# Attention maxima placed in two runs of 512 queries a unit, with earlier loads, column groups in the router and head copies in halves

## What is computed

```python
x = x + attention0(layernorm(x))     # 16 heads of 16, softmax over 1024 keys, k mixed from its two halves
x = x + ffn0(layernorm(x))           # 256 -> 1024 -> 256, ternary weights, a low-rank part, squared relu
x = x + statespace1(layernorm(x))    # a linear recurrence a feature, layernorm, gelu, projection
x = x + experts1(layernorm(x))       # 16 experts, the 2 best of each token, 256 -> 512 -> 256
```

```python
attn = jnp.einsum('bhqc,bhkc->bhqk', q, k_eff) * scale
attn = softmax(attn, axis=-1)
out  = jnp.einsum('bhqk,bhkd->bhqd', attn, v)
...
logits = jnp.einsum('sbd,de->sbe', x, Wg) + bg + bias
vals, idx = top_k(logits, 2)
```

## Time and profile before

| what | before |
|---|---|
| median of 3 runs | 1851.45 us (1850.39 to 1857.02) |
| the profiled execution | 1850.05 us, span in the profile 1848.3 us |
| projection, to the first matmul of attention | 0 to 122.2 us |
| attention | 122.2 to about 856 us |
| PE, DVE, ACT, POOL busy | 85%, 66%, 54%, 23% of the span |
| mean granted PE clock | 0.916 of full speed |

### The profile page before, as it was taken

How to read it: one execution, slowest core, us unless ns; L and a number is a source line. 1 busy time by engine, 2 the same in 40 slices (tenths; PEclk the granted TensorE clock), 3 DMA queues, 4 the chain that set the end, 5 groups by cost and what they waited for, 6 DMA issues and landing times. The chain is left out here.

```text
span 1848.3 us, 39878 instructions
## 1 busy us (share of the span) xinstructions
PE 1569.6 (85%) x13929; PEld 1028.1 (56%) x13930; DVE 1215.2 (66%) x2121; ACT 991.2 (54%) x2005; POOL 432.0 (23%) x569
## 2 busy tenths in 40 slices
PE   5949999999999999998789976889787299999990
PEld 4824333333333333334678865878674189888880
DVE  6639999999999999911478867666656822222225
ACT  2410888888888888883154422333223145554442
POOL 2119000000000000000112126222212355555550
PEclk9965999999999999997899986999897599999995
DMA  5682133333333443000100001332209432222118
GB/s 180 221 193 36 27 55 57 42 54 42 55 51 53 67 58 58 9 20 16 15 1 1 1 13 48 94 93 77 65 2 310 145 105 66 67 65 65 62 63 275
DMA packets 117613, 135.14 MB, mean 73 GB/s; under 512 B 27028, under 2 KB 91560, under 8 KB 117352
## 3 DMA queue, kind: packets, MB, share of 16 engines
q1 hardware_dynamic: 104712, 107.60, 25.1%
q0 software_dynamic: 7584, 20.72, 3.5%
q10 hardware_dynamic: 5184, 4.98, 0.8%
HBM read 92.23 MB, written 36.04 MB: 69 GB/s over the span
## 5 line engine op out<-in xcount | busy, mean ns | idle before, releaser
L1862 DVE TENSOR_REDUCE mx<-ps 128x1 f32<-128x1024 f32 x512 | 616.7, 1220 | 39.6 <-PE ps L1984 37.8
L1901 ACT ACTIVATE PR<-ps 128x512 f32<-128x512 f32 x1024 | 559.9, 595 | 140.3 <-PE ps L2026 74.3
L1984 PE MATMUL ps<-KQ 48*128 48x512 f32 x1024 | 393.3, 468 | 30.6 <-PEq L238 24.2
L2026 PE MATMUL ps<-KQ 50*128 50x512 f32 x1024 | 374.6, 445 | 0.0
L2010 PE MATMUL ps<-PR,VO 128*32 128x256 f32 x4096 | 328.2, 392 | 31.9 <-ACT OT L1891 31.5
L2026 PEld LDWEIGHTS ps<-KQ 50*128 50x128 f32 x1024 | 153.1, 186 | 211.0 <-ACT PR L1901 204.5
L2010 PEld LDWEIGHTS ps<-PR,VO 128*32 128x32 f32 x4096 | 81.7, 108 | 219.9 <-ACT PR L1901 121.1
L1984 PEld LDWEIGHTS ps<-KQ 48*128 48x128 f32 x1024 | 160.2, 196 | 60.8 <-DVE mx L1862 35.0
L1742 PE MATMUL ps<-eW,e_hiddenT 128*128 x632 | 155.4, 389 | 5.1 <-DVE e_hiddenT L1719 2.6
L1752 PEld LDWEIGHTS ps<-e_xinT,e_w 128*128 128x128 f32 x1264 | 154.9, 193 | 5.7 <-issue 1.7
L1752 PE MATMUL ps<-e_xinT,e_w 128*128 128x128 f32 x1264 | 155.5, 277 | 1.1 <-ACT e_xinT L1684 1.1
(11 more groups left out here) (276 smaller groups left out, 2160.0 us busy)
## 6 DMA issues: line engine op xcount, KB each, us to landing
KQ<-qk_parts SPq DMA_DIRECT2D x192, 128.0 KB, 6.0
qk_parts<-parts SPq DMA_DIRECT2D x8, 2048.0 KB, 6.9
TB<-toeplitz_lines SPq DMA_DIRECT2D x32, 512.0 KB, 5.5
eW<-in_L_ffn_W SPq DMA_DIRECT2D x16, 512.0 KB, 7.1
eW<-in_L_ffn_W SPq DMA_DIRECT2D x8, 1024.0 KB, 12.2
e_got<-expert_outputs SPq DMA_DIRECT2D x16, 512.0 KB, 10.2
X<-in_L_attn_x SPq DMA_DIRECT2D x8, 512.0 KB, 4.4
V<-OT SPq DMA_DIRECT2D x64, 64.0 KB, 6.5
```

What stands on the lines that cost most here:

```text
L1862: nc.vector.tensor_reduce(mx[:, u % RING, h * QT + q:h * QT + q + 1], ps[:, b:b + 2].rearrange("p a n -> p (a n)"), AX, ALU.max, negate=Tr ...
L1901: nc.scalar.activation(PR[:, kt % 2, h], ps[:, st_bank(u, s)], ACT.Exp).then_inc(exp_done, 1)
L1984: made = nc.tensor.matmul(ps[:, max_bank(u, t) + k], kq[half(h, KROWS), 1, h % HR, q * P:(q + 1) * P], kq[half(h, KROWS), 0, h % HR, k * B ...
L2026: nc.tensor.matmul(ps[:, st_bank(u, s)], kq[half(h, AROWS), 0, h % HR, kt * P:(kt + 1) * P], kq[half(h, AROWS), 1, h % HR, qc * BANK:(qc + ...
```

## The change

- **Early loads.** SP stores all chunks in one loop, and issues half of `load_qk` of unit 0 after the store of chunk 2 and the other half after chunk 3, and unit 1's after chunks 4 and 5. Nothing is left ahead of the stores of chunks 6 and 7.
- **Queries in two runs.** The query side of `KQ` is laid out by run of 512 queries, then head. `load_qk` has 6 transfers of 128 KB for the keys and 12 of 64 KB for the queries (pieces of 2 KB in place of 4 KB).
- **Maxima in two runs.** `negated_rows` comes after every 16th tile (`AHEAD`), for one run, on half as many columns. `rows(u, qc)` has 8 transfers of half the size for each run. PE waits for the rows of a run ahead of that run's first block. 16 + 12 tiles stand ahead of the first block of all. SP's order in a unit: `load_qk(u + 2)`, `heads(u - 1)`, `rows(u, 1)`, `rows(u + 1, 0)`, `spread_inverses`.
- **Heads in two copies.** `keep_heads` copies 256 queries at a time, after the first and the third exponential of the next step. PE waits for the first copy ahead of part 1 of the last step's `weigh`, and for both ahead of the next step's part 0.
- **Router in column groups.** `wg` is widened to 32 columns with zeros, which POOL writes ahead of its load. Each of a chunk's four token tiles has its own 32 partitions of the result (8 matmuls of 128 tokens in place of 2 of 512), ACT copies 128 x 128, and one matmul with 64 columns turns it back in place of four.

```diff
+                            FIRST_STORED = SEQ // CW
+                            for c in range(NC):
+                                h = c % 2
                                 sp.wait_ge(lo_ready, 2 * DK * (c + 2))
                                 sp.dma_start(pqk[...], parts[...]).then_inc(stored[h], 16)
-                            chunks(sp, body)
+                                u, second = divmod(c - FIRST_STORED, 2)
+                                if 0 <= u < 2:
+                                    for h2 in range(2):
+                                        sp.wait_ge(stored[h2], 16 * 2)
+                                    load_qk(sp, u, u, range(second * QK_LOADS // 2, (second + 1) * QK_LOADS // 2))
...
             for u in range(UNITS):
                 for t in range(MAXES):
                     reduce(u, t)
-                negated_rows(u)
+                    if (t + 1) % AHEAD == 0:
+                        negated_rows(u, t // AHEAD)
...
-                    if kt == 1 and h == 0:
-                        if step > KT:
-                            keep_heads(u, 0)
+                    if kt == 0 and h % 2 == 0:
+                        if step > 0:
+                            keep_heads(u, 0, h // 2)
                         elif u > 0:
-                            keep_heads(u - 1, 1)
+                            keep_heads(u - 1, 1, h // 2)
...
                 if u > 0:
                     heads(u - 1)
+                rows(u, 1)
                 if u + 1 < UNITS:
-                    rows(u + 1)
+                    rows(u + 1, 0)
...
+                kept_before = WPARTS * (QC * u + step // KT)
+                if kt == 0 and part == 0 and kept_before > 0:
+                    pe.wait_ge(ot_kept, kept_before)
+                if kt == KT - 1 and part > 0:
+                    pe.wait_ge(ot_kept, kept_before + part)
...
-            for t in range(MAXES + LEAD):
+            for t in range(AHEAD + LEAD):
...
-                    ahead = MAXES * (u + 1) + t + LEAD
+                    ahead = MAXES * u + AHEAD + t + LEAD
...
                         for dk in range(DK):
-                            last = nc.tensor.matmul(ps[0:E, 5 + h, 0:CW], wg[:, dk], xT[:, h, dk], ...)
+                            for k in range(CT):
+                                last = nc.tensor.matmul(ps[LANES * k:LANES * (k + 1), 5 + h, 0:P], wg[:, dk], xT[:, h, dk, k * P:(k + 1) * P], ...)
...
-                        for k in range(CT):
-                            last = nc.tensor.matmul(ps[:, 4, ds(E * (CT * c + k), E)], lT[h][:, k * P:(k + 1) * P], ident[0:E, 0:E], ...)
+                        nc.tensor.matmul(ps[:, 4, ds(CT * E * c, CT * E)], lT[h], lanes_of, ...)
```

More of the change, by code:

```diff
@@ L201, in transformer_kernel, with load_qk @@
                 KQ = [sbuf(st, f"KQ{r}", [P, 2, HR, SEQ], F32R) for r in range(2)]
+                queries = lambda r: KQ[r][:, 1].rearrange("p h n -> p (h n)").rearrange("p (b h n) -> p b h n", b=QC, n=BANK)
                 kq_loaded = [sem(f"kq_loaded{r}") for r in range(RING)]
-                def load_qk(sp, u, r):
+                K_LOADS = 2 * len(PAIR_K)
+                QK_LOADS = K_LOADS + QC * 2 * len(PAIR_Q)
+                def load_qk(sp, u, r, some=range(QK_LOADS)):
                     b, g = u // UPB, u % UPB
                     src = pqk.rearrange("s a k p t -> s a (k p) t").rearrange("s a (g h c) t -> s a g c h t", h=HG, c=HD)
[L208 to L213, removed]
+                    for n in some:
+                        j, y = n // 2 % len(PAIR_Q), n % 2
+                        row = HALF * y + HD * j
+                        if n < K_LOADS:
+                            to, side, part, start, width = KQ[r][row:row + HD, 0], 1, PAIR_K[j], 0, SEQ
+                        else:
+                            qc = n // K_LOADS - 1
+                            to, side, part, start, width = queries(r)[row:row + HD, qc], 0, PAIR_Q[j], BANK * qc, BANK
+                        sp.dma_start(to.bitcast(F32),
+                                     src[side, part, ds(g, 1), :, HR * y:HR * (y + 1), ds(SEQ * b + start, width)].rearrange("g c h t -> (g c) h t")).then_inc(kq_loaded[r], 16)
                 with ExitStack() as s1:
@@ L1578, in body @@
                         for dk in range(DK):
-                            last = nc.tensor.matmul(ps[0:E, 5 + h, 0:CW], wg[:, dk], xT[:, h, dk], start=(dk == 0), stop=(dk == DK - 1))
+                            for k in range(CT):
+                                last = nc.tensor.matmul(ps[LANES * k:LANES * (k + 1), 5 + h, 0:P], wg[:, dk], xT[:, h, dk, k * P:(k + 1) * P],
+                                                        start=(dk == 0), stop=(dk == DK - 1))
                         last.then_inc(lt_done, 1)
@@ L1955, in _ @@
             ffw.load(sp)
-            rows(0)
+            rows(0, 0)
             for u in range(UNITS):
@@ L1983, in first_pass @@
                 kq = KQ[u % RING]
-                made = nc.tensor.matmul(ps[:, max_bank(u, t) + k], kq[half(h, KROWS), 1, h % HR, q * P:(q + 1) * P],
+                made = nc.tensor.matmul(ps[:, max_bank(u, t) + k], of_tile(queries(u % RING), h, q),
                                         kq[half(h, KROWS), 0, h % HR, k * BANK:(k + 1) * BANK], start=True, stop=True)
@@ L1995, in again @@
                     pe.wait_ge(red_done, min(ahead - PAIRS + 1, MAXES * UNITS))
-                nc.tensor.matmul(ps[:, MAX_BANK + 2 * (ahead % PAIRS) + k], kq[half(h, KROWS), 1, h % HR, q * P:(q + 1) * P],
+                nc.tensor.matmul(ps[:, MAX_BANK + 2 * (ahead % PAIRS) + k], of_tile(queries((UNITS - 1) % RING), h, q),
                                  kq[half(h, KROWS), 0, h % HR, k * BANK:(k + 1) * BANK], start=True, stop=True)
@@ L2011, in weigh @@
                                             start=(kt == 0 and part == 0), stop=(kt == KT - 1), skip_group_check=True)
[L2012 to L2015 removed]
+                last.then_inc(pv_done, 1)
+            for t in range(AHEAD + LEAD):
                 for k in range(QC):
```

103 lines of the change are left out of this document (51 added, 52 removed).

## The result

The changed kernel takes 1795.2 us, median of 4 runs (1787.7 to 1806.6), against 1853.6 us for the kernel before in the same session: a ratio of 0.970, with a 95% interval of 0.967 to 0.973. The forecast was 1798 us. The profiled execution takes 1793.0 us with a span of 1791.3 us, 57.0 us less than the span before, where the sum gave 53.4.

A forecast was written before the change was run, and what follows sets the result against it. Attention was taken to be paced by PE. Terms of -12.2, -20.3, -18.6, +5.2 and -7.5 gave -53.4, from 1850.05 to 1796.7 us, and with the median 1.4 above the profiled run 1798; range 1786 to 1820.

The forecast's parts named there:

- Early loads: End of projection: first loads of q and k fill gaps between stores, so attention starts earlier; -12.2 us, bounds -10 and -17.6.
- The bound of -17.6: End of projection: loads and stores overlap so far that only the last store remains; -17.6 us in place of -12.2.
- bytes count and not pieces: Transfers of queries: pieces of 2 KB have no fixed cost as a rule, since stores move such pieces at 410 GB/s.
- Sixteen fewer tiles: Ahead of attention's first block: 16 tiles at 1.267 us no longer stand ahead; -20.3 us, bounds 19.5 and 21.
- Heads in two copies: `weigh` in attention: PE loses 0.49 us in place of 1.09 at the copy; -18.6 us, between 0 and -28.
- The rival without effect: Copies of heads: ACT waits twice for PE, so a stall of 1.09 us stays; 1817 us, chance 0.09.
- More negations: Attention: two negations in a unit, 0.28 us each instead of 0.22 once; +5.2 us, bounds 3 and 15.
- SP's queue: Second run's rows in attention: they fit by 0.4 to 1.1 us, so 0 us; bounds 0 and +30.
- "even" for `spread_inverses`: SP in every other unit: its inverse is done at +40.4, where `load_qk` is wanted, so no loss.
- the bytes ahead of it are the same: SP's queue ahead of the second run's rows: 12 us of loads and 2 of heads, done by +14.5.
- The first rival's price: Second run's rows: land 1 to 3 us late in 15 units; 1813 to 1843 us, chance 0.17.
- Router: Last chunk's logits in the router: ready earlier after DVE's normalizing; -7.5 us, bounds 6 and 9.

The follow-up runs named there:

- e3: The changed kernel with the first pass's loads issued where the kernel before issued them: 1812.7 us, ratio 0.977.
- e7: The changed kernel with the maxima in one run, both negations after all 32 tiles and 44 tiles ahead of the first block: 1810.1 us, ratio 0.977.
- e2: The changed kernel with the heads of a run copied at once, as before: 1813.2 us, ratio 0.979.
- e1: The changed kernel with SP issuing `heads(u - 1)` and `rows(u, 1)` ahead of `load_qk(u + 2)`: 1800.2 us, ratio 0.971.
- e5: The changed kernel with six more 64 B transfers on SP ahead of the second run's rows in each unit: 1936.9 us, ratio 1.043.
- e4: The changed kernel with the router's column groups undone: 1805.7 us, ratio 0.973.
- e8: The changed kernel with rows issued ahead of the loads, as in e1, and `LEAD` 8 instead of 12: 1785.5 us, ratio 0.962.
- e12: The same version as e9, run again beside the changed kernel on one chip: 1786.7 us, ratio 0.965.
- e9: The changed kernel with rows ahead of the loads, `LEAD` 8 and POOL's multiplication behind the negation: 1782.8 us, ratio 0.963.
- e6: The changed kernel with only POOL's multiplication of the heads moved behind the second run's negation: 1802.2 us, ratio 0.972.

## Why the prediction was right, and where it was not

**Early loads: -18.5 instead of -12.2, the size was off.** The sum let stores and loads follow one another at their separate rates. The rows after show 298 to 392 GB/s in most stretches that hold both, where loads alone have 130 and a store alone 410: a queue that holds both isn't as slow as the sum of the two. The bound of -17.6, "only the last store remains", was the right reading. (By the sum's own terms the store of chunk 5 lands at 52.3 + 4 x 5.4 + 3 x 6 = 91.9, not at 94.4; nothing rests on it.) The prediction's "bytes count and not pieces" was its own reading of the port rule; e3 bears it out, since loads of which two thirds are cut in 2 KB pieces weren't slower. By e3, 15.5 us of it come from where the loads stand. The other 3 go with their smaller transfers; that these cause it was not tested alone.

**Sixteen fewer tiles: -20.4 against -20.3.** e7 takes them back for +20.8. The rows of the first run were in time, as worked out.

**Heads in two copies: -20.5 (e2) against -18.6**, with the stall of 0.42 against 0.49. The rival without effect is out, and so is its second wait at part 1.

**More negations: +1.6 (e2) against +5.2.** A negation of half the columns costs 0.16 us, not 0.28, where I had let each cost more than the one long negation did; why it hides better was not tested. The trace before couldn't show a collision with POOL: there no step of it ran beside the multiplication. In e1 one did, and took 2.03 us.

**SP's queue: 0 was wrong.** The text called it the term that it trusted least, with 0.4 to 1.1 us to spare. In the three profiles of the changed kernel PE waits 4.1, 6.0 and 3.9 us in five to seven units. Two steps of the term failed. One is the issue time: in most units an issue of `heads` takes 1.1 to 1.9 us, and the issues of the worst unit took 1.5 us more than I had summed. The other is "even" for `spread_inverses` and "the bytes ahead of it are the same": behind it the loads begin 0.2 to 0.3 us later (265.92 is 0.16 ahead of the unit's first block, 225.02 is 0.48), and its 512 KB share the queue, which is full until 15 to 16 us after the first load where it is 9 to 13 in the other units. Which units wait goes with the second, 14 of 18 times, and not with the slow issues; that issue time counts too is what e5 shows. How much of a wait each is worth was not tested: no run moves L195 alone. The first rival's price (1 us late in all 15 units) didn't come: only five to seven units wait at all, most of them behind L195.

**Router: -7.0 instead of -7.5.** e4 gives back 7.4 us (12.8 against 5.4).

**What no term had: the clock.** One turn takes 2.16 us at the lower level (`weigh` starts at 182.93 and 185.09 in the kernel before) and 1.23 at the upper, so each us at the lower level loses 0.43. It came in two places. Behind a wait of 1.61 us, the interval was 5.3 us longer; behind the long waits of the second profile, 3.8 and 4.9; in the third, whose longest wait was 1.1 us, none was. And the clock rises 9.2 us after the first block in the kernel before (178.87 to 188.1), and 13.5 and 24.4 us after it in the first and third profile after. By 0.43 that is 1.8 and 6.5 us more than before.

So the second pass of the first profile adds up: -18.9 (31 intervals of 20.27 in place of 20.88), +4.1 waits, +5.3 clock behind one of them, and +3.4 for the later rise of the clock (1.8) and the two ends of the pass (1.6, which is what was left and wasn't taken apart): -6.1. The forecast was close by luck: the late rows and the clock cost some 11 us that it had at nothing, and the loads' extra 6 us, the cheaper negation and the copies (5.5 together), and 5 us that no term had, made up for it. These 5 us of the 57, in the untouched stretches of the table, weren't taken apart; the third profile has 558.1 and 424.3 us there.

**Left open.** Why the clock takes between 9 and 46 us after the first block to rise (45 in e2, 29 in e8, 22 in e9, 46 in e12) with PE busy 4.00 of 4.00 us in nearly every stretch of it (e2 alone has two, of 3.57 and 3.60). It differs between executions of one kernel too (13.5, 13.7 and 24.4 us), and at 0.43 us for each, 37 us of difference are 16 us of time, as much as many of the spreads above. Keeping PE busy across the waits wasn't tried. Nor is it settled why e1 alone, without any wait for rows, has the median of the changed kernel: its one profile shows one collision that costs something, 6.3 us, but not how often it comes in the other runs. The times of its runs go with their mean granted clock (1787.8 us at 0.921, 1808.8 at 0.907, 1838.3 at 0.891).

## What to carry to other kernels

When a moved transfer fits its deadline by less than a few of its queue's issue times, price the lateness twice: the wait, and TensorE at the lower clock behind it, which here cost nothing after some waits and up to six times the wait (e4) after others. Count the queue's bytes unit by unit, not for a typical unit: a transfer that comes every other unit stood ahead of 14 of the 18 waits. Then order the queue by deadline, the small late transfers ahead of the big early ones. That removed every wait (e1) but no time from the median by itself; with a shorter lead the medians fell by 14 us (e8), and with a third change by 8 (e12), each against the changed kernel on the same chip. The lead accounts for 5.1; what gave the rest isn't shown. Transfers that wait at a stage's end are best issued in the gaps of the transfers before it; bound them from below by the last one alone.

## What the runs showed of the hardware

- Waits of PE of 1.3 to 1.8 us were followed, in six of these profiles, by a stretch at 1.2 GHz that lengthened one interval by 3.8 to 9.7 us. Not always: e2 has a wait of 1.6 us in an interval of 22.63 us, which is 20.93 and the wait, and of e3's waits of 1.39, 1.45 and 1.81 us only the last was followed by a long one (9.7 us). No wait of the third profile, 1.1 us at most, had it. Before the change the 1.02 us waits, one every 21 us, left the clock at 1.00.
- Issues on SP take 0.45 to 0.66 us as a rule, and one of the eight of `heads` took 1.25 to 1.77 in 11 of 13 units of the first profile.
- The 2 KB transfers of the rows landed late in units whose loads follow the 512 KB of L195 in the same queue: the last was issued by 372.7 us (by 698.3 in the second profile), and the block that waits for them starts at 375.5 (701.9). In a unit without these 512 KB the last was issued by 244.7, and the block at 245.8 doesn't wait.
- A negation step of 128x16 takes 0.17 us, and 2.0 to 2.4 (e1, e2, e4, e5 and the first profile) when POOL's 2.38 us multiplication of 128x1024 began just before it. With the multiplication behind the negation (e6) none is over 0.6.
- 3 MB of loads in 64 KB and 128 KB transfers ran at 140 to 157 GB/s (e3), and in 128 KB transfers alone at 125 to 132. Between stores most stretches of 4 us had 298 to 392 GB/s together with these.
